# Adjacency build of a graph network: the source one-hots of four blocks interleaved, and loaded as weights with a step of four elements

## The reference

```python
edge_index = jnp.stack([src, dst])
h = jnp.maximum(_layernorm(x, axis=-1), 0.0)
x = x + _L0_gnn_ref(h, edge_index, ...)
    # agg_sum = segment_sum(x[src], dst); aggs = agg_sum / maximum(cnt, 1)
...
x = x + _L3_gnn_ref(h, edge_index)
    # ten times: agg = segment_sum(norm * xk[src], dst)
```

## Time and profile before

| | |
|---|---|
| time, median of 3 runs | 4933.57 us (4926.85 to 4945.77) |
| span of the profiled execution | 6157.9 us |
| time of the profiled execution beyond its span | not recorded; the span is what is known of it |
| build loop, first to last ACT copy of a tile | 89.1 to 617.4 us |
| TensorE's mean granted clock over the span | 0.844 of full speed |
| busy shares of the span | PE 73%, PEld 46%, DVE 41%, ACT 17%, POOL 53% |

### The profile page before, as it was taken

One profiled execution on the slowest core, in us unless ns is written; L12 is line 12 of the kernel. 1 busy time (PEld: TensorE's weight loads), 2 busy tenths in 40 slices (PEclk: granted clock), 3 DMA queues, 4 the chain that ended last, 5 costly groups with the idle time before them and its releaser, 6 DMA issues.

```text
span 6157.9 us, 72323 instructions
## 1 busy us (share of the span) xinstructions
PE 4502.8 (73%) x25760; PEld 2814.8 (46%) x25760; DVE 2553.7 (41%) x8838; ACT 1022.9 (17%) x2922; POOL 3237.6 (53%) x3390
## 2 busy tenths in 40 slices
PE   3778477888775445446555788988888898888888
PEld 2556355566554334344444343434443444444344
DVE  6778444445443445555567422222222222222222
ACT  4656311111111000001222200000000000000001
POOL 3232365566555555555553365565656556565655
PEclk8888688899887666667767999989999999999999
DMA  5222222122222222222221555555555555555554
GB/s 136 77 83 79 77 56 52 51 58 59 55 55 57 67 70 75 68 68 69 65 71 42 160 173 159 171 158 164 172 167 164 166 178 166 161 174 161 165 170 135
DMA packets 455501, 686.46 MB, mean 111 GB/s; under 512 B 91793, under 2 KB 237879, under 8 KB 455120
## 3 DMA queue, kind: packets, MB, share of 16 engines
q1 hardware_dynamic: 341188, 454.71, 23.5%
q0 software_dynamic: 107584, 223.83, 14.0%
q10 hardware_dynamic: 6364, 3.20, 0.2%
HBM read 599.50 MB, written 82.31 MB: 111 GB/s over the span
## 4 chain that ended last, share of the span: by engine, by line
PE 42%; another core or an unknown queue 24%; DVE 18%; issue 11%; ACT 3%; DMA 1%; ACTq 0%; SPq 0%; DVEq 0%; POOL 0%; POOLq 0%
PE ps L2007 27%; PE ps L1751 5%; DVE E L2458 4%; DVE B L2538 2%; PE pt L2102 2%; DVE arena L2580 1%; PE ps L1828 1%; PE ps L2093 1%; PE pt L2038 1%; PE ps L2022 1%; DVE O L3023 1%; PE pt L1719 1%; ACT E L1561 1%; DVE scores L3019 1%
## 5 line engine op out<-in xcount | busy, mean ns | idle before, releaser
L2007 PE MATMUL ps<-arena,E 128*128 128x512 fp8e4 (+1 forms) x4900 | 1147.0, 385 | 93.6 <-issue 84.8
L2007 PE MATMUL ps<-arena,A 128*128 128x512 fp8e4 (+1 forms) x4900 | 1142.1, 385 | 62.4 <-issue 60.1
L1052 POOL DMA_INDIRECT arena<-table,src_i x810 | 776.9, 959 | 685.7 <-DMA table<-E 255.0
L1017 POOL DMA_INDIRECT E<-gat_table,src_i x782 | 759.3, 971 | 634.6 <-DVE arena L2580 367.7
L1052 POOL DMA_INDIRECT arena<-x_spill,src_i x810 | 775.3, 957 | 579.0 <-issue 225.8
L1002 POOL DMA_INDIRECT arena<-table,src_i x782 | 742.8, 950 | 583.5 <-issue 217.1
L1751 PE MATMUL ps<-E,arena 128*128 128x352 f32 (+22 forms) x2932 | 783.6, 421 | 241.1 <-DVE E L2458 155.4
L2007 PEld LDWEIGHTS ps<-arena,E 128*128 128x128 f16 x4900 | 471.4, 100 | 648.6 <-issue 193.9
L2007 PEld LDWEIGHTS ps<-arena,A 128*128 128x128 f16 x4900 | 472.9, 100 | 608.9 <-issue 154.8
L1751 PEld LDWEIGHTS ps<-E,arena 128*128 128x128 f32 x2932 | 515.4, 211 | 441.4 <-issue 195.5
L2909 DVE SCALAR_TENSOR_TENSOR C<-ps,sc_b,scores 128x128 f32<-128x128 f32 x490 | 138.9, 345 | 1295.1 <-PE ps L2022 769.3
(11 more groups left out here) (350 smaller groups left out, 4557.6 us busy)
## 6 DMA issues: line engine op xcount, KB each, us to landing
arena<-adj SPq DMA_DIRECT2D x180, 1024.0 KB
arena<-adj SPq DMA_DIRECT2D x90, 1088.0 KB
adj<-E SPq DMA_DIRECT2D x39, 784.0 KB
arena<-table,src_i POOLq DMA_INDIRECT x1592
O<-dst_rows SPq DMA_DIRECT2D x112, 224.0 KB
arena<-adj SPq DMA_DIRECT2D x20, 768.0 KB
x_spill<-A SPq DMA_DIRECT2D x55, 256.0 KB
arena<-x_spill,src_i POOLq DMA_INDIRECT x810
```

Source lines behind the costliest of these rows:

```text
L1017: pool.indirect_dma_start(out=att_rows[:, b % 3 * AB + at, :], out_offset=None, in_=gat_table, in_offset=bass.IndirectOffsetOnAxis(ap=src_ ...
L1052: pool.indirect_dma_start(out=y_rows[:, g % ERING, k, :], out_offset=None, in_=(table, x_spill)[half], in_offset=bass.IndirectOffsetOnAxis ...
L2007: mm = pe.matmul(chunk_banks[n % 2][:, 0:len(some) * P], y[:, i, h * D:(h + 1) * D], adj_ring[:, piece % ADJ_RING, 0:len(some), at:at + P] ...
```

## The change

The source one-hots of four blocks lie side by side: for each low source part n the four blocks' values are neighbours, block number innermost. A second table, `iota_beside`, holds 0,0,0,0,1,1,1,1 to 127 and is written once at the start by one more DVE copy. The comparison then reads `iota_beside` and the four edges' low bits, the row of four repeated 128 times, and no operand has an innermost step of 0. PE reads a block's 128 weights with a step of four elements (8 bytes). Everything else, with its order and its waits, stays.

```diff
+        iota_beside = arena[:, MARK + 448:MARK + 448 + SRC_AT_ONCE * P // 2].bitcast(BF16).rearrange("p (n s) -> p n s", s=SRC_AT_ONCE)
...
-        hot_src = scores.rearrange("p t f -> p (t f)")[:, 0:SRC * P // 2].bitcast(BF16).rearrange("p (s n) -> p s n", s=SRC)
+        hot_src = scores.rearrange("p t f -> p (t f)")[:, 0:SRC * P // 2].bitcast(BF16).rearrange("p (g n s) -> p g n s", n=P, s=SRC_AT_ONCE)
...
-                            pe.matmul(ps[pair % 4][:, h * BW:(h + 1) * BW], hot_src[:, g % SRC, :],
+                            pe.matmul(ps[pair % 4][:, h * BW:(h + 1) * BW], hot_src[:, g % SRC // SRC_AT_ONCE, :, g % SRC_AT_ONCE],
                                       hot_code[:, g % HOT, 0:BW], start=True, stop=True).then_inc(sem("built"), 1)
...
             dve.tensor_copy(iota_h, iota_i[:, 0:P])
+            dve.tensor_copy(iota_beside, bc(iota_i[:, 0:P], SRC_AT_ONCE))
             link(dve.tensor_copy(iota_w, iota_i[:, :]))
...
-                            dve.tensor_tensor(hot_src[:, g % SRC:g % SRC + SRC_AT_ONCE, :], row_bc(iota_h, SRC_AT_ONCE),
-                                              bc(slot_lo[:, g // P, g % P:g % P + SRC_AT_ONCE], P), ALU.is_equal)
+                            dve.tensor_tensor(hot_src[:, g % SRC // SRC_AT_ONCE, :, :], iota_beside,
+                                              row_bc(slot_lo[:, g // P, g % P:g % P + SRC_AT_ONCE], P), ALU.is_equal)
```

## The result

The changed kernel takes 4886.22 us (median of 6 runs, 4885.20 to 4886.56) against 4931.68 us before (6 runs, 4926.85 to 4947.32): 0.9881 of it, 95% interval 0.9856 to 0.9906. 45.5 us are gone; 40 were forecast.

A forecast was written before the change was run, and what follows sets the result against it. DVE bounds undisturbed build-loop rounds at 10.07 us; DVE's 8.48 falls below the ACT/PE floor 8.75, plus 0.2 gives 8.95. 37 rounds x 1.12 = 41, taken as 40: 4933.6 - 40 = 4894 us; own range 4880 to 4908, 8-in-10 range 4870 to 4934.

The forecast's parts named there:

- 0.35 us by the rate of the code one-hot: Source one-hots on DVE: 512 elements fall from 0.60 to 0.35 us, saving 1.63 us a round.
- Rounds of 10.07: Build loop before the change: undisturbed rounds take 10.07 us, bound by DVE, whose own work sums to 10.11.
- the floor of 8.75: Build loop: ACT and PE at their own pace need 8.75 us a round, next to be late behind DVE.
- The 0.2: Build loop: 0.2 us a round added for DVE, ACT and PE tripping each other, estimated from their gap of 0.27.
- the sign of an ACT busy for over 48 of 50 us: Sign of being right: in undisturbed stretches ACT is busy over 48 of 50 us, with rounds of 8.8 to 9.2.
- I take 0: PE's weight load with a step: no added cost taken; the ends were 0 and 3.0 us a round.
- The 54 ns of cover: PE: six matmuls of 110 ns in a 0.66 us pair leave a load some 54 ns before it shows.
- (c): PE, line 2093: the stepped weight load becomes the bound; at four times its clocked part +62 us, 4996; chance 0.11.
- (d): PE's weight load grows to between two and three times, losing part of the gain, 4905 to 4934; chance 0.07.
- the rounds that a faster DVE cannot help: Build loop: about eleven stalled rounds, each followed by a recovery round, where a faster DVE gains nothing.
- 17%: Build loop: share of the profile's unexplained releases kept in a timed run, 254 us, some two of eleven stalled rounds.
- the forecast of 40: Whole kernel: 37 rounds at 1.12 us less each give 41, taken as 40 us saved; chance 0.60.

The follow-up runs named there:

- compare_slow: Changed kernel, but the comparison reads its table with each element repeated by an innermost step of 0; 4966.85 us, 0.9996 of the kernel before.
- before_again: The kernel before, no edit, profiled a second time; 4980.74 us, span 4978.6.
- no_row_sums: Changed kernel, but ACT's copy of a pair does not sum, so its accumulator read goes; 4889.68 us.
- step12: Changed kernel with all three groups of the ring interleaved, so weights load with a step of 12 elements (24 bytes); 4889.36 us.
- group 3: Runs sharing one chip, among them after_filled and before_third; there the kernel before took 4960.6 us in the median, the changed kernel 4885.65.
- group 1: Runs sharing another chip, among them before_again and compare_slow; there the kernel before took 4970.8 us in the median, the changed kernel 4889.22.
- after_filled: Changed kernel with every second block's code one-hot written by two instructions instead of one; 4928.59 us, 0.9937 of the kernel before.
- before_third: The kernel before, no edit, profiled a third time; 4983.09 us, span 4981.2.
- before_one_port: The kernel before, its code one-hot reading a table of five rows of 49 with gaps; 4981.49 us, 1.003 of the kernel before.

## Why the prediction was right, and where its working was not

The time, 4894 forecast and 4886 measured, came by the steps that were given for the comparison, DVE and the load; two terms behind them were right by luck.

**The comparison.** 0.35 us by the rate of the code one-hot; 0.33 measured, the exact halving. That it was the operand's innermost step and nothing else in the layout is shown by compare_slow. The Trainium skill's rule ("Vector Engine (DVE) Microarchitecture Reference", section 5.1) held in both halves: one element read again and again goes at one a cycle (676 ns), a row of four read again and again at two (416).

**DVE last before, PE and ACT behind it.** Rounds of 10.07 read from the earlier trace rows, 9.99 measured in the 35 ordinary rounds of before_again; the floor of 8.75 plus 0.2 gave 8.95, and 8.94 was measured. The 0.2 is luck. It was put in for three engines that trip each other, and what was measured is PE's own work: 8.75 came from a round with four edge-by-edge matmuls, and the others are longer by 0.11 us for each one more (no_row_sums). That PE and not ACT is the floor, the prediction left open; no_row_sums shows it, and the sign of an ACT busy for over 48 of 50 us was missed (46.98 and 47.47).

**The weight load.** "I take 0" was right for the kernel and wrong for the load: 113 ns, and 142 at a step of 12. What made it right is that a load hides beside matmuls, and 46 ns more of it still do (step12). The 54 ns of cover are not confirmed: they rest on reading the longest load as one whose clocked part takes twice as long, and by that reading step12 (142 in the median, 168 at the longest) would have a clocked part of only 26 ns, not one that grew. The Trainium skill's rule on lines ("Advanced Engine Details and Errata", section SBUF Cachelines) does not agree with the trace: with two hits a line it says full speed, and the load took 17 ns more. Rivals (c) and (d) had the right place; the size of the step's cost was too small for them.

**The step that failed: the rounds that a faster DVE cannot help.** The prediction took the standstills of the earlier trace rows, which come while POOL gathers, as rounds that DVE does not bound, let 17% of them stay, and said that there "a faster DVE gains nothing". In that profile the longest gather is 1.58 us, so that long gathers were not behind its standstills; what was, stays open. The executions after that show neither those standstills nor, in the changed kernel, any stalled round but the one that waits for the first rows. What the two later profiles of the kernel before have is another thing: three rounds of about 30 us each, with gathers of 8 to 10 us ahead of them. The faster comparison removes them, and by medians that was worth 32 us in group 3; in group 1 the two profiles differ by 55.5 us in long rounds. On the first chip it was little: the median before, 4931.7, lies 3 us above after_filled's 4928.6. So the forecast of 40 fits the 45.5 there by ordinary rounds alone (1.13 x 37 = 42 us, and after_filled shows 42.9), and if few long rounds came into that measurement, that is luck too; no profile of a timed run there shows their number.

**What holds the gathers.** Shown: they become long with the slow comparison and the fast code one-hot together (before_again, before_third, compare_slow). They do not with the code one-hot slowed (before_one_port), nor with the comparison fast, code one-hots split and DVE just as full (after_filled). The Trainium skill's page "SBUF — State Buffer", section "SBUF: two separate sides", says that POOL cannot write a gather's descriptors while DVE runs an operation that uses two ports at once, and that the shared ports are held for a whole instruction. The kernel before and before_one_port agree with it: the edit takes that form from the code one-hot, by the rule that its expectation names, and the long gathers go. But by the rule after_filled, whose DVE has no gap (50.00 of 50 us) and spends more of a round on such operations (10.1 us less 2.1 for the comparisons, against 10.0 less 3.9; an estimate), should hold POOL up as well, and its longest gather is 1.31 us. So it is not the whole rule.

At which moment POOL gets in can be read from the three traces, though no run tests it. Of their 32 gathers of over 4 us, 24 end 0.83 to 0.84 us after DVE begins to finish a tile (line 2978; 2980 in compare_slow), once a round. The other eight end 0.81 or 0.82 us after DVE's last instruction before it stands still. Two of the 24, in before_again: the gather of 258.98 ends at 263.77 and that of 264.07 at 273.46, and DVE's rows there are

```profile
262.87 0.14 DVE L2977 TENSOR_SCALAR cnt<-arena 128x1 f32<-128x1 f32 x1
262.94 0.27 DVE L2978 TENSOR_TENSOR C<-pt,arena 128x128 f32<-128x128 f32 x1
263.13 0.46 DVE L3023 TENSOR_SCALAR O<-arena 128x245 bf16<-128x245 bf16 x2
263.52 0.68 DVE L3019 TENSOR_TENSOR scores<-arena 128x512 bf16<-128x512 bf16 x1
...
272.57 0.14 DVE L2977 TENSOR_SCALAR cnt<-arena 128x1 f32<-128x1 f32 x1
272.63 0.27 DVE L2978 TENSOR_TENSOR C<-pt,arena 128x128 f32<-128x128 f32 x1
272.83 0.67 DVE L3019 TENSOR_TENSOR scores<-arena 128x512 bf16<-128x512 bf16 x1
```

Whether code one-hots or a comparison come next makes no difference, so by the timing it is the finishing that these gathers wait for. The rows also show how the rhythm keeps itself up: POOL starts its next gather 0.30 us after such an end, which puts it some 0.55 or 0.94 us behind the start of a comparison (264.07 and 273.77 here, the first long again, the second not), and 17 of the 23 gathers that start so are long. Of the 176 gathers that start 0.03 to 0.49 us behind one, with DVE just as full, none takes over 1.47 us; those of 237.13 and 238.51 are among them. Why these places shut POOL out and others do not, stays open.

## What to carry to other kernels

Look at the innermost step of every operand of an all-16-bit two-input operation: a step of 0 in one of them halves the rate of the whole, and repeating a row instead of an element avoids it, here at the price of weights with a step, which stayed hidden behind matmuls. Before reading waits off a profile, compare its span with the timed runs: where it is a quarter longer, take instruction durations from it and no waits. And when the engine that everyone waits for gets faster, look for what it was holding up besides: here the gathers of another engine, which are the likely reason that the old kernel's time wanders by 75 us.

## What was not expected of the hardware

A weight load's time grows with the step of its columns: 96 to 97 ns at one element, 113 at four (8 bytes), 142 at twelve (24 bytes), for 128 bf16 columns. A gather by POOL of 0.94 to 1.1 us can last 8 to 10 us beside a full DVE, for several in a row, or not at all, depending on which operations DVE repeats and on where between them the gather starts. And a bf16 comparison against a per-partition number, 245 columns, takes 336 ns when its input lies in five rows of 49 with gaps (before_one_port) and 275 when it lies in one run (before_again).
